# Entering the second graph layer of a four-layer network: paired projection, early aggregation, and float16 parts made elsewhere

## The chip, the cores and the metric

One core of one Trainium2 chip runs the whole program. The metric is device time in microseconds, from one launch. TensorE multiplies matrices, VectorE, ScalarE and GpSimd (POOL in the profile) do the elementwise work, SyncE (SP) issues most transfers. Each engine works through its own instruction list in order; they meet at semaphores.

## The reference

2048 nodes with 256 features; `adj` is a 2048 x 2048 matrix of zeros and ones. Four graph layers, each with a residual and a layer norm. The change lies between the first and the second:

```python
# layer 0: attention over the graph
e = where(adj > 0, h @ h.T, -9e15);  edge_att = softmax(e, axis=1)
x = layernorm(x + adj * (node_att * edge_att) @ (x @ weight) + bias)
# layer 1
type_sum = adj @ x                       # for both gates, and for (adj @ x) @ W_gcnb
attn_a, attn_b = sigmoid([type_sum, x] @ Wa.T + ba), sigmoid([type_sum, x] @ Wb.T + bb)
h = x @ W_sa
scores = (h @ a_left)[:, None] + (h @ a_right)[None, :]
e = where(adj != 0, exp(-leaky_relu(scores, 0.01)), 0)
x = layernorm(x + sigmoid(attn_a * (e / (e.sum(1) + 1e-5)) @ h + attn_b * (adj @ (x @ W_gcnb) + b_gcnb)))
# layers 2 and 3: two more graph convolutions, each with residual and layer norm
```

## The kernel before

**Numbers and parts.** A float32 product is made from a high and a low part of each operand (three products). `adjT`, the transposed adjacency, is bfloat16 and exact, so products with it need only the two parts of the other side. `x16` holds float16 high and low parts of 2048 times x.

**Layer 0, rounds of one row tile (128 rows, T = 16 tiles).** In round t (`round0`, `scores`, `weighted`) TensorE makes the 128 x 2048 scores in banks 0 to 3, VectorE adds the mask and takes the maxima in two halves (`maxima`, `masked_max`), ScalarE takes the exponential (`exp_row`) and the float16 high part of P (`p_high`), VectorE the low part (`p_low`), SyncE transposes both by DMA, and TensorE sums P times support (`weighted`) in bank 6 or 7, two rounds later. VectorE then does `final0` for tile t-3 (residual and moments), POOL the factor 1/sqrt(var) (`norm_factor`), VectorE the norm (`normed`), which gives the tile of x that layer 1 needs.

**The entry of layer 1.** Of each tile of x POOL makes the float16 high part (`conv_high`, line 455), VectorE the low part (`conv_first`, line 1183). TensorE transposes a pair of tiles (`turn16`, line 610, banks 4 and 5 in turn), ScalarE copies the result (`turned_read`, line 898; three kept), TensorE projects tile by tile (`project16`, line 625, banks 0 to 3): h, and in four more columns s_left, s_right and x's share of the two gates. ScalarE takes v = exp(-0.01 s_right) (line 902) and H_hi = v h (line 903), VectorE `ex` (line 1188) and H_lo (line 1189). A projection of tile t waits for both parts of tile t-4. When all 16 are through, `left_row` (line 637) spreads s_left over all partitions for 512 columns at a time, in banks 6 and 7.

**Layer 1 proper**, in four blocks b of 512 nodes. `aggregate_tiles` (line 664) adds adj times x over 16 tiles jt in banks 4 and 5 (4 matmuls a tile). Per pair of tiles: `edge_scores` on VectorE (lines 1278, 1281), two exponentials on ScalarE (`edge_exp`, lines 929, 930), `edge_low` on VectorE (line 1082), `attend` on TensorE (line 689, 24 matmuls). Each pair of attention has some aggregated tiles ahead of it; in block 0 that list is `AGG_FIRST = (8, 2, 2, 2, 1, 1)`, so all of block 0's aggregation stands behind the projection. After the sixth pair `neighbours` projects the aggregate.

**Memory.** `x16` lies over the adjacency's staging buffers `adjb` (high parts over buffers 0 and 1, low parts over 2 and 3), so conversions start only when the last mask (`fill_ready`, ScalarE's `make_fill`, line 850) and the adjacency's transposes are through.

**Orders written out by hand.** All of this stands in each engine's list in a fixed order. On POOL, `conv_high(0..6)` stands at the end of round t = 11 and 7..11 at the end of t = 12. POOL's and VectorE's rounds are those of tile t, which finishes three rounds of TensorE's later.

Of the kernel before, what the change touches and what calls it, by code (L numbers as in the profile page):

```python
# [23 lines left out]
ALU = mybir.AluOpType  # L24
# [46 lines left out]
def build(nc, x_in, adj_in, w0_in, b0_in, node_in, edge_in, wsa_in, asa_in, wg_in, bg_in,  # L71
# [31 lines left out]
    AGG_FIRST = (8, 2, 2, 2, 1, 1)  # L103
# [9 lines left out]
    with ctx:  # L113
# [193 lines left out]
        t16_mm, t16_read, sl_mm, sl_read = sem("t16_mm"), sem("t16_read"), sem("sl_mm"), sem("sl_read")  # L307
        p1_mm, p1_hi, p1_lo, ex_ready = sem("p1_mm"), sem("p1_hi"), sem("p1_lo"), sem("ex_ready")
# [93 lines left out]
        def _(pool):  # L402
# [45 lines left out]
            def conv_high(t):  # L448

                if t == 0:  # L450
                    pool.wait_ge(fill_ready, T)
                    for k in range(AB):
                        pool.wait_ge(adjT_landed[k], 16 * (T // AB))
# [68 lines left out]
        def _(pe):  # L522
# [78 lines left out]
            def turn16(g):  # L601

                pe.wait_ge(conv_lo, 2 * g + 2)
                if g >= 2:
                    pe.wait_ge(t16_read, g - 1)
                for i in range(2):
                    for part in (HI, LO):
                        for k in range(KD):
                            q = (2 * i + part) * KD + k
                            ins = nc.tensor.transpose(bank16(4 + g % 2)[:, q * P:(q + 1) * P],  # L610
                                                      x16[:, part, 2 * g + i, k * P:(k + 1) * P], identb[:, :])
                ins.then_inc(t16_mm, 1)

            def project16(t):

                if t == 0:
                    pe.wait_ge(w16_ready, 1)
                    pe.wait_ge(e_read, 2 * T)
                if t >= 4:
                    pe.wait_ge(p1_hi, t - 3)  # L620
                    pe.wait_ge(p1_lo, t - 3)
                pe.wait_ge(t16_read, t // 2 + 1)
                for k in range(KD):
                    for p, q in ((HI, HI), (HI, LO), (LO, HI)):
                        ins = mm(bank(t % 4, D + 4), turned16(t, p, k), w16[:, q, k, :],
                                 start=(k == 0 and (p, q) == (HI, HI)), stop=(k == KD - 1 and p == LO))
                ins.then_inc(p1_mm, 1)

            def left_row(b):

                if b == 0:
                    pe.wait_ge(p1_lo, T)
                    pe.wait_ge(pv_read, T)
                if b >= 2:
                    pe.wait_ge(sl_read, b - 1)
                for k in range(TB):
                    ins = nc.tensor.transpose(ps[:, 6 + b % 2, k * P:(k + 1) * P],
                                              ex[:, b * TB + k, 1:2].to_broadcast([P, P]), ident[:, :])
# [12 lines left out]
            left_row(0)  # L651
            left_row(1)
# [27 lines left out]

            def attend(b, pair):
# [17 lines left out]
            def block1(b):  # L699


                first, tiles = 0, AGG_TILES if b else AGG_FIRST
                wait_from(pe, g_ev, b * TB)
                for pair in range(PAIRS):
                    if pair < len(tiles):
                        for jt in range(first, first + tiles[pair]):
                            for f in range(KD):
                                aggregate_tiles(0, b, f, (jt,))
                            if b == 0 and jt == 3:
                                left_row(2)  # L710
                                left_row(3)
                        first += tiles[pair]
                    if b == 0 and pair == 0:
                        pe.wait_ge(H_ready, 2)
                    attend(b, pair)
# [5 lines left out]
            for k in range(AB):  # L721
                pe.wait_ge(adjT_landed[k], 16 * (T // AB))
# [106 lines left out]
        def _(act):  # L829
# [57 lines left out]
            for t in range(2, T):  # L887
                exp_row(t)
                p_high(t)
                if t + 2 < T:  # L890
                    make_fill(t + 2)
            def turned_read(g):
# [3 lines left out]
                if g >= KEPT:  # L896
                    act.wait_ge(p1_mm, 2 * (g - KEPT) + 2)
                run(xT16[:, g % KEPT, :], bank16(4 + g % 2), ACT.Copy).then_inc(t16_read, 1)

            def projected(t):  # L900
                act.wait_ge(p1_mm, t + 1)
                own.link(run(vj[:, t, :], ps[:, t % 4, D:D + 1], ACT.Exp, scale=gw[:, 4:5]))
                run(H[HI][:, t, 0:D], bank(t % 4, D), ACT.Copy, scale=vj[:, t, :]).then_inc(p1_hi, 1)

            def left_row(b):
                act.wait_ge(sl_mm, b + 1)
                run(slrow[:, b * CB:(b + 1) * CB], bank(6 + b % 2), ACT.Copy).then_inc(sl_read, 1)
# [58 lines left out]

            edge_exp(0, 0)
            left_row(2)
            left_row(3)
            edge_exp(0, 1)  # L970
# [99 lines left out]
        def _(dve):  # L1070
# [109 lines left out]
            def conv_first(tiles):  # L1180
                for t in tiles:
                    dve.wait_ge(conv_hi, t + 1)
# [3 lines left out]
            def projected(t):  # L1186
                dve.wait_ge(p1_hi, t + 1)
                own.link(ts(ex[:, t, :], ps[:, t % 4, D:D + 4], gw[:, 3:4], None, ALU.mult))
                stt(H[LO][:, t, 0:D], bank(t % 4, D), vj[:, t, :], H[HI][:, t, 0:D].bitcast(F32),
                    ALU.mult, ALU.subtract).then_inc(p1_lo, 1)  # L1190

            def round0(t):

                u = t % 2
                maxima(t, u)
                if t >= 3:
                    final0(t - 3, 1 - u)
                if t == T - 1:
                    conv_first(range(3))
# [55 lines left out]
            dve.wait_ge(H_ready, 1)  # L1255
            low(H[LO][:, :, D:D + 1], vj[:, :, :], H[HI][:, :, D:D + 1]).then_inc(H_ready, 1)
# [107 lines left out]
            for k in range(AB):  # L1364
                dve.wait_ge(adjT_landed[k], 16 * (T // AB))
            dve.wait_ge(sl_read, 1)
# [153 lines left out]
```

## Time and profile before

| | |
|---|---|
| runs (us) | 831.36, 829.05, 848.21; median 831.36 |
| profiled execution | 831.39 |
| its span, first to last instruction | 829.6 |
| TensorE busy | 775.2 (93%) |
| VectorE busy | 447.0 (54%) |
| ScalarE busy | 333.3 (40%) |
| POOL busy | 115.5 (14%) |
| mean granted clock of TensorE | 0.986 |

Times in rows are microseconds from the span's start. Layer 0 ends and layer 1 begins between about 204 and 260. Matmuls are pipelined: the duration of one includes its way through the array, so work is counted by the distance from one start to the next. In brackets stands an engine's idle time ahead of the instruction, and what ended it.

### The profile page before, as it was taken

How to read it: one execution, taken by the hardware profiler on the slowest of the kernel's cores; microseconds unless marked ns; L12 is line 12 of the kernel's file. 1: busy time of each engine (PE TensorE's matmuls, PEld its weight loads, DVE VectorE, ACT ScalarE, POOL GpSimd, SP SyncE). 2: the span in 40 equal slices, each digit the busy share in tenths (PEclk: the TensorE clock that was granted, in tenths of full speed). 3: DMA queues.
4: the chain of work that ended last, by engine and by line, in shares of the span. 5: the costliest groups of instructions: out<-in, count | busy, mean ns of one | idle time of the engine just before them, and what ended most of it. 6: DMA issues, size and time to landing. Idle time of an engine off the chain costs nothing.

```text
span 829.6 us, 11863 instructions
## 1 busy us (share of the span) xinstructions
PE 775.2 (93%) x4247; PEld 511.4 (62%) x4288; DVE 447.0 (54%) x937; ACT 333.3 (40%) x499; POOL 115.5 (14%) x214
## 2 busy tenths in 40 slices
PE   7898989899979999999979999999988999997997
PEld 6776656666656978686835554665663456464443
DVE  4586667477867778787873354221225111112655
ACT  4575536554465464646541142331335222223100
POOL 1012111112730001010111120000002000000343
PEclk9999999999989999999999999999999999999999
DMA  8979999995400000000011000000000000000011
GB/s 226 184 128 172 181 180 173 171 200 100 90 1 14 1 1 1 1 2 1 1 32 52 0 1 0 1 0 0 0 1 25 1 1 0 0 0 1 19 39 44
DMA packets 112572, 42.41 MB, mean 51 GB/s; under 512 B 103312, under 2 KB 109584, under 8 KB 112528
## 3 DMA queue, kind: packets, MB, share of 16 engines
q1 hardware_dynamic: 110224, 33.44, 20.6%
q0 software_dynamic: 2304, 8.39, 6.5%
q8 instruction: 27, 0.44, 0.2%
q14 instruction: 17, 0.14, 0.1%
HBM read 22.95 MB, written 2.10 MB: 30 GB/s over the span
## 4 chain that ended last, share of the span: by engine, by line
issue 40%; PE 35%; DVE 7%; SPq 6%; POOL 4%; DMA 4%; ACT 4%; POOLq 0%; ACTq 0%; DVEq 0%
PE ps L664 10%; PE ps L817 6%; PE ps L767 5%; SPq L365 4%; PE ps L571 3%; PE ps L754 3%; DMA turned<-pl 2%; PE ps L530 2%; SPq L358 2%; PE ps L583 2%; POOL rstd L417 1%; PE ps L553 1%; ACT em L855 1%; DVE em L1124 1%; PE ps L585 1%
## 5 line engine op out<-in xcount | busy, mean ns | idle before, releaser
L664 PE MATMUL ps<-adjT,x 128*128 128x512 bf16 (+1 forms) x739 | 168.5, 379 | 8.4 <-DVE x L1361 4.3
L664 PEld LDWEIGHTS ps<-adjT,x 128*128 128x128 f16 x768 | 71.8, 98 | 91.0 <-issue 5.6
L583 PE MATMUL ps<-sup,turned 128*128 128x512 f16 x256 | 85.7, 385 | 4.4 <-DMA turned<-pl 3.8
L1082 DVE TENSOR_TENSOR hh_lo<-hf,hh_hi 128x512 fp32r<-128x512 f32 x32 | 22.1, 692 | 116.6 <-ACT hf L1028 116.6
L789 PE MATMUL ps<-adjT,G 128*128 x375 | 82.6, 379 | 0.9 <-ACT hf L1028 0.4
L689 PE MATMUL ps<-H_hi,es_hi 128*128 128x258 f32 x256 | 76.8, 300 | 2.1 <-DVE es_lo L1082 1.7
L689 PE MATMUL ps<-H_hi,es_lo 128*128 128x258 f32 x256 | 72.4, 283 | 0.0
L689 PE MATMUL ps<-H_lo,es_hi 128*128 128x258 f32 x256 | 72.4, 283 | 0.0
L585 PE MATMUL ps<-sup,turned 128*128 128x256 f16 x256 | 70.6, 276 | 0.0
L416 POOL TENSOR_TENSOR rstd<-mv,epsc 128x1 f32<-128x1 f32 x64 | 14.6, 227 | 369.6 <-DVE mv L1096 361.8
L789 PEld LDWEIGHTS ps<-adjT,G 128*128 128x128 f16 x384 | 37.3, 98 | 45.4 <-issue 0.9
L817 PE MATMUL ps<-x,adjT 128*128 128x512 f16 x256 | 58.1, 387 | 3.7 <-DVE x L1465 3.7
L1133 DVE SCALAR_TENSOR_TENSOR pl<-em,ph 128x1024 f16<-128x1024 f32 x32 | 40.2, 1297 | 39.3 <-DMA turned<-pl 31.1
L571 PE MATMUL ps<-hT_hi 128*128 128x512 f32 x128 | 52.1, 407 | 6.1 <-DVE mx L1124 4.6
L855 ACT ACTIVATE em<-em,negm 128x2048 f32<-128x2048 f32 x16 | 32.1, 2004 | 63.8 <-DVE negm L1156 63.8
L929 ACT ACTIVATE es_hi<-tm 128x1024 fp32r<-128x1024 f32 x32 | 33.9, 1058 | 57.8 <-DVE tm L1281 55.7
L689 PEld LDWEIGHTS ps<-H_hi,es_hi 128*128 128x128 f32 x256 | 48.4, 189 | 6.8 <-DVE es_lo L1082 4.2
L571 PE MATMUL ps<-hT_hi,hT_lo 128*128 128x512 f32 x128 | 50.7, 396 | 0.0
L571 PE MATMUL ps<-hT_lo,hT_hi 128*128 128x512 f32 x128 | 50.4, 394 | 0.0
L689 PEld LDWEIGHTS ps<-H_lo,es_hi 128*128 128x128 f32 x256 | 48.5, 189 | 0.5
L583 PEld LDWEIGHTS ps<-sup,turned 128*128 128x128 f16 x256 | 25.3, 99 | 38.0 <-issue 9.3
L689 PEld LDWEIGHTS ps<-H_hi,es_lo 128*128 128x128 f32 x256 | 48.3, 189 | 0.0
(196 smaller groups left out, 1439.8 us busy)
## 6 DMA issues: line engine op xcount, KB each, us to landing
adjb<-in_adj POOLq DMA_DIRECT2D x16, 512.0 KB, 7.4
x<-in_x SPq DMA_DIRECT2D x4, 512.0 KB, 6.1
out<-adjf SPq DMA_DIRECT2D x16, 128.0 KB, 1.7
adjf<-in_L_gnn_W SPq DMA_DIRECT2D x1, 1024.0 KB, 5.4
W1f<-in_L_gnn_W SPq DMA_DIRECT2D x1, 512.0 KB, 3.7
adjf<-in_L_gnn_W SPq DMA_DIRECT2D x1, 512.0 KB, 3.8
we<-in_L_gnn_edge_w SPq DMA_DIRECT2D x1, 256.0 KB, 3.8
w0x<-in_L_gnn_weight SPq DMA_DIRECT2D x1, 256.0 KB, 7.0
```

What stands on the lines that cost most here:

```text
L365: sp.dma_start_transpose(PT(part, t % 2), (ph, pl)[part][:, :]).then_inc(PT_landed[part], 16)
L571: ins = mm(bank(c), hT[p][:, k, t * P:(t + 1) * P], hT[q][:, k, c * CB:(c + 1) * CB], start=(k == 0 and (p, q) == (HI, HI)), stop=(k == KD ...
L583: ins = mm(bank(6 + u), PT(HI, u)[:, jt, :], sup[:, jt, :], start=(jt == 0), stop=False, skip_group_check=True)
L585: ins = mm(bank(6 + u, D), PT(LO, u)[:, jt, :], sup[:, jt, 0:D], start=False, stop=(jt == T - 1), skip_group_check=True)
L664: ins = mm(bank(4 + f), x16[:, part, jt, f * P:(f + 1) * P], adj(b, jt), start=(jt == 0 and part == HI), stop=(jt == T - 1 and part == LO))
L689: ins = mm(bank(k, D + 2), es[p][:, (b * T + jt) % RE, k * P:(k + 1) * P], H[q][:, jt, :], start=(jt == 0 and (p, q) == (HI, HI)), stop=(j ...
L767: ins = mm(bank(2 + k % 2, width), hh[p][:, o, k * P:(k + 1) * P], ws[q][:, o, :], start=(o == 0 and (p, q) == (HI, HI)), stop=(o == KH - ...
L789: ins = mm(bank(4 + o), g16(jt, part, o * P, P), adj(b, jt), start=(jt == 0 and part == HI), stop=(jt == T - 1 and part == LO))
L817: ins = mm(bank(u), adjT[:, bass.ds(b, 1), jt, k * P:(k + 1) * P].rearrange("p a c -> p (a c)"), f16[:, jt, :], start=(jt == 0), stop=(jt ...
L855: run(em[:, t % 2, :], em[:, t % 2, :], ACT.Exp, bias=negm[:, t:t + 1], accum_out=Z[:, t:t + 1]) \
L929: own.link(run(es[HI][:, s, :], tm[:, s, :], ACT.Exp, scale=SLOPE - 1.0))
L1133: stt(pl[:, cols], em[:, u, cols], TOP, ph[:, cols], ALU.mult, ALU.subtract).then_inc(p_lo, 1)
```

## The change

1. **High parts.** Tiles 0 to 12 are converted by ScalarE: 0 to 6 after its last fill, 7 to 10 a round later, 11 and 12 after the last. POOL keeps 13 to 15, each right after its own tile's factor.
2. **Low parts** by VectorE: 0 to 2 between the halves of round 14's maxima, 3 and 4 before its P low part; 5 to 7 and 8 and 9 likewise in round 15; 10 to 15 among the last final steps.
3. **Projection in pairs** (`project16(g)`), with a semaphore `ex_made` for VectorE's columns. `projected(0)` and `projected(1)` stand earlier on VectorE. The last weighted sum stands after the first pair, not after the second.
4. **Early aggregation.** Between pairs, TensorE aggregates tiles 0 to 7 of block 0 (`agg_early`), so transposes go to banks 4, 5, 6, 6, 6, 7, 6, 6 (`TURN_BANK`). `AGG_FIRST` becomes (2, 2, 1, 1, 1, 1).
5. **Left row 0** is made after the fifth pair, and the first edge scores and exponentials of block 0 stand before the last projected parts on VectorE and ScalarE.

```diff
+    CONV_ROUND = {T - 2: (range(0, 3), range(3, 5)), T - 1: (range(5, 8), range(8, 10))}
+    TURN_BANK = (4, 5, 6, 6, 6, 7, 6, 6)
+    AGG_EARLY = 8
-    AGG_FIRST = (8, 2, 2, 2, 1, 1)
+    AGG_FIRST = (2, 2, 1, 1, 1, 1)
...
 # GpSimd
-                if t == T - 5:
-                    for c in range(7):
-                        conv_high(c)
-                if t == T - 4:
-                    for c in range(7, 12):
-                        conv_high(c)
                 if t >= T - 3:
-                    conv_high(t - 1)
-            conv_high(T - 1)
+                    conv_high(t)
...
 # TensorE, turn16
-                if g >= 2:
-                    pe.wait_ge(t16_read, g - 1)
+                if g == 2:
+                    pe.wait_ge(pv_read, T - 1)
+                if g == 5:
+                    pe.wait_ge(pv_read, T)
+                if to in TURN_BANK[:g]:
+                    pe.wait_ge(t16_read, max(n for n in range(g) if TURN_BANK[n] == to) + 1)
...
-            def project16(t):
+            def project16(g):
...
-                if t >= 4:
-                    pe.wait_ge(p1_hi, t - 3)
-                    pe.wait_ge(p1_lo, t - 3)
-                pe.wait_ge(t16_read, t // 2 + 1)
-                for k in range(KD):
+                if g >= 2:
+                    pe.wait_ge(p1_hi, 2 * g - 2)
+                    pe.wait_ge(p1_lo, 2 * g - 2)
+                    pe.wait_ge(ex_made, g - 1)
+                pe.wait_ge(t16_read, g + 1)
+                for t in (2 * g, 2 * g + 1):
...
             def left_row(b):
+                pe.wait_ge(ex_made, 2 * b + 2)
                 if b == 0:
-                    pe.wait_ge(p1_lo, T)
-                    pe.wait_ge(pv_read, T)
-                if b >= 2:
-                    pe.wait_ge(sl_read, b - 1)
+                    pe.wait_ge(t16_read, 6)
+                if b == 2:
+                    pe.wait_ge(t16_read, TURNS)
+                if b % 2:
+                    pe.wait_ge(sl_read, (b + 1) // 2)
...
-            weighted(T - 2)
-            turn16(0)
-            for g in range(1, TURNS):
-                if g == 3:
-                    weighted(T - 1)
-                turn16(g)
-                project16(2 * g - 2)
-                project16(2 * g - 1)
-            project16(T - 2)
-            project16(T - 1)
-            left_row(0)
-            left_row(1)
+            def agg_early(*jts):
+                for jt in jts:
+                    if jt == 0:
+                        pe.wait_ge(t16_read, 2)
+                        for k in range(AB):
+                            pe.wait_ge(adjT_landed[k], 16 * (T // AB))
+                    for f in range(KD):
+                        aggregate_tiles(0, 0, f, (jt,))
+
+            weighted(T - 2)
+            turn16(0)
+            turn16(1)
+            project16(0)
+            weighted(T - 1)
+            for g in range(1, TURNS - 1):
+                turn16(g + 1)
+                project16(g)
+                agg_early(g - 1)
+                if g == 4:
+                    left_row(0)
+            project16(TURNS - 1)
+            agg_early(TURNS - 2, TURNS - 1)
+            left_row(1)
...
 # TensorE, block1: left_row(2), left_row(3) stand before attend(0, 0), which also waits for p1_lo
...
 # ScalarE
+            def conv_high(tiles):
+                for t in tiles:
+                    if t == 0:
+                        act.wait_ge(fill_ready, T)
+                        for k in (0, 1):
+                            act.wait_ge(adjT_landed[k], 16 * (T // AB))
+                    act.wait_ge(y_normed, t + 1)
+                    run(x16[:, HI, t, :], x[:, t, :], ACT.Copy, scale=XS).then_inc(conv_hi, 1)
...
+                if t == T - 3:
+                    conv_high(range(7))
+                if t == T - 2:
+                    conv_high(range(7, 11))
+            conv_high(range(11, 13))
...
-            turned_read(0)
-            for g in range(1, TURNS):
-                turned_read(g)
-                projected(2 * g - 2)
-                projected(2 * g - 1)
-            projected(T - 2)
-            projected(T - 1)
-            run(H[HI][:, :, D:D + 1], vj[:, :, :], ACT.Copy).then_inc(H_ready, 1)
-            left_row(0)
-            left_row(1)
+            turned_read(0)
+            turned_read(1)
+            projected(0)
+            for g in range(1, TURNS - 1):
+                turned_read(g + 1)
+                projected(g)
+                if g == 4:
+                    left_row(0)
             edge_exp(0, 0)
+            projected(TURNS - 1)
+            column(0, T)
+            left_row(1)
+            edge_exp(0, 1)
             left_row(2)
             left_row(3)
-            edge_exp(0, 1)
...
 # VectorE
-            def maxima(t, u):
+            def maxima(t, u, between=()):
                 dve.wait_ge(fill_ready, t + 1)
                 masked_max(t, u, 0)
+                conv_first(between)
                 masked_max(t, u, 1)
...
+            def projected(g):
+                two, at = slice(2 * g, 2 * g + 2), 2 * (g % 2)
+                dve.wait_ge(p1_hi, 2 * g + 2)
+                ts(ex[:, two, :], ps[:, at:at + 2, D:D + 4], gw[:, 3:4], None, ALU.mult).then_inc(ex_made, 1)
+                for i in range(2):
+                    t = 2 * g + i
+                    stt(H[LO][:, t, 0:D], bank(at + i, D), vj[:, t, :], H[HI][:, t, 0:D].bitcast(F32),
+                        ALU.mult, ALU.subtract).then_inc(p1_lo, 1)
...
-            conv_first(range(3, 10))
+            conv_first(range(10, 12))
             final0(T - 3, 1)
-            conv_first(range(10, 12))
+            conv_first(range(12, 13))
             normed(T - 3, 1, x[:, T - 3, :])
-            conv_first(range(12, 13))
...
             final0(T - 2, 0)
             conv_first(range(13, 14))
+            projected(0)
             normed(T - 2, 0, x[:, T - 2, :])
-            for t in range(4):
-                projected(t)
+            conv_first(range(T - 2, T - 1))
             final0(T - 1, 1)
-            conv_first(range(T - 2, T - 1))
+            projected(1)
             normed(T - 1, 1, x[:, T - 1, :])
-            for t in range(4, 6):
-                projected(t)
+            projected(2)
             conv_first(range(T - 1, T))
-            for t in range(6, T):
-                projected(t)
+            for g in range(3, 6):
+                projected(g)
...
             dve.wait_ge(sl_read, 1)
             edge_scores(0, 0)
+            projected(TURNS - 2)
             edge_scores(0, 1)
+            projected(TURNS - 1)
+            dve.wait_ge(H_ready, 1)
+            low(H[LO][:, :, D:D + 1], vj[:, :, :], H[HI][:, :, D:D + 1]).then_inc(H_ready, 1)
```

## Rows read from the trace of the kernel before

**Rows 1.** The page's first part: busy time of each engine, share, instructions.

```profile
PE 775.2 (93%) x4247; PEld 511.4 (62%) x4288; DVE 447.0 (54%) x937; ACT 333.3 (40%) x499; POOL 115.5 (14%) x214
```

**Rows 2.** Busy time by stretch: length, engines' busy us, clock, DMA share, GB/s.

```profile
219.00:258.40 39.40, 32.51 (x244) 23.10 (x243) 26.56 (x77) 24.95 (x49) 12.92 (x16) 0.91 0.10 24
260.00:410.00 150.00, 147.06 (x1026) 121.08 (x1040) 124.00 (x232) 81.74 (x108) 11.69 (x24) 1.00 0.00 1
```

**Rows 3.** Timeline of TensorE, 219 to 262: start, busy, line, shapes, idle before.

```profile
219.45 1.06 PE L610 MATMUL ps<-identb,x 128*128 128x128 f16 x16
221.26 1.49 PE L625 MATMUL ps<-adjf,xT 128*128 128x260 f16 x12 [0.76 <-ACT xT L898]
222.59 0.61 PE L610 MATMUL ps<-identb,x 128*128 128x128 f16 x8
223.04 1.50 PE L625 MATMUL ps<-adjf,xT 128*128 128x260 f16 x12
224.37 0.38 PE L583 MATMUL ps<-sup,turned 128*128 128x512 f16 x1
...
229.57 0.61 PE L610 MATMUL ps<-identb,x 128*128 128x128 f16 x8
232.14 1.59 PE L625 MATMUL ps<-adjf,xT 128*128 128x260 f16 x12 [1.96 <-issue]
...
239.72 0.49 PE L625 MATMUL ps<-adjf,xT 128*128 128x260 f16 x3 [2.20 <-issue]
...
249.84 1.09 PE L637 MATMUL ps<-ident,ex 128*128 128x128 f32 x8 [1.83 <-DVE H_lo L1189]
250.98 3.40 PE L664 MATMUL ps<-adjT,x 128*128 128x512 bf16 x15
...
258.36 0.47 PE L689 MATMUL ps<-H_hi,es_hi 128*128 128x258 f32 x1
...
261.68 1.67 PE L664 MATMUL ps<-adjT,x 128*128 128x512 bf16 x7
```

**Rows 4.** Busy time by stretch, three more stretches; the third last column is the clock.

```profile
221.00:222.00 1.00, 0.74 (x7) 0.68 (x8) 0.93 (x3) 1.00 (x2) 0.92 (x2) 1.00 0.32 63
232.20:237.00 4.80, 4.80 (x34) 3.78 (x35) 3.73 (x12) 3.22 (x7) 0.51 (x2) 0.64 0.01 2
240.00:250.00 10.00, 8.08 (x65) 6.30 (x63) 7.17 (x23) 7.41 (x19) 3.32 (x2) 0.83 0.00 0
```

**Rows 5.** Timeline of VectorE before two of TensorE's pauses end.

```profile
230.64 0.42 DVE L1183 SCALAR_TENSOR_TENSOR x<-x 128x256 f16<-128x256 f32 x1 [1.89 <-POOL x L455]
...
231.56 0.48 DVE L1189 SCALAR_TENSOR_TENSOR H_lo<-ps,vj,H_hi 128x256 fp32r<-128x256 f32 x1
...
239.14 0.48 DVE L1189 SCALAR_TENSOR_TENSOR H_lo<-ps,vj,H_hi 128x256 fp32r<-128x256 f32 x1
```

**Rows 6.** Timeline, VectorE and ScalarE: rounds 14 and 15, and later conversions.

```profile
200.19 2.01 ACT L855 ACTIVATE em<-em,negm 128x2048 f32<-128x2048 f32 x1 [4.62 <-DVE negm L1156]
...
209.38 1.22 DVE L1124 CUSTOM_DVE_ANT_0 em<-ps,fill 128x1024 f32<-128x1024 f32 x1 [1.31 <-PE ps L571]
...
217.47 2.49 DVE L1183 SCALAR_TENSOR_TENSOR x<-x 128x256 f16<-128x256 f32 x6
...
495.51 1.38 ACT L981 ACTIVATE x<-x 128x256 f16<-128x256 f32 x4
```

**Rows 7.** Timeline, ScalarE and VectorE: copies, scaled copies, and one pair's edges.

```profile
220.09 1.94 ACT L898 ACTIVATE xT<-ps 128x1024 f16<-128x1024 f16 x2 [5.00 <-PE ps L610]
222.42 0.47 ACT L903 ACTIVATE H_hi<-ps,vj 128x256 fp32r<-128x256 f32 x1
...
251.72 1.42 DVE L1281 SCALAR_TENSOR_TENSOR tm<-slrow,ex,nb 128x512 f32<-128x512 f32 x2
...
253.17 1.06 ACT L929 ACTIVATE es_hi<-tm 128x1024 fp32r<-128x1024 f32 x1 [1.55 <-DVE tm L1281]
...
255.42 1.23 DVE L1082 TENSOR_TENSOR es_lo<-tm,es_hi 128x1024 fp32r<-128x1024 f32 x1 [0.37 <-ACT tm L930]
```

More of the change, by code:

```diff
@@ L448, in conv_high @@
             def conv_high(t):
[L450 to L453, printed above, removed]
                 pool.wait_ge(y_normed, t + 1)
@@ L609, in turn16 @@
                             q = (2 * i + part) * KD + k
-                            ins = nc.tensor.transpose(bank16(4 + g % 2)[:, q * P:(q + 1) * P],
+                            ins = nc.tensor.transpose(bank16(to)[:, q * P:(q + 1) * P],
                                                       x16[:, part, 2 * g + i, k * P:(k + 1) * P], identb[:, :])
                 ins.then_inc(t16_mm, 1)
-            def project16(t):
-                if t == 0:
+            def project16(g):
+                if g == 0:
@@ L627, in project16 @@
+                pe.wait_ge(t16_read, g + 1)
+                for t in (2 * g, 2 * g + 1):
+                    for k in range(KD):
+                        for p, q in ((HI, HI), (HI, LO), (LO, HI)):
+                            ins = mm(bank(t % 4, D + 4), turned16(t, p, k), w16[:, q, k, :],
+                                     start=(k == 0 and (p, q) == (HI, HI)), stop=(k == KD - 1 and p == LO))
                 ins.then_inc(p1_mm, 1)
             def left_row(b):
+                pe.wait_ge(ex_made, 2 * b + 2)
@@ L699, in block1 @@
             def block1(b):
-                first, tiles = 0, AGG_TILES if b else AGG_FIRST
+                first, tiles = (0, AGG_TILES) if b else (AGG_EARLY, AGG_FIRST)
                 wait_from(pe, g_ev, b * TB)
@@ L708, in block1 @@
                                 aggregate_tiles(0, b, f, (jt,))
-                            if b == 0 and jt == 3:
-                                left_row(2)
-                                left_row(3)
                         first += tiles[pair]
                     if b == 0 and pair == 0:
+                        left_row(2)
+                        left_row(3)
                         pe.wait_ge(H_ready, 2)
+                        pe.wait_ge(p1_lo, T)
                     attend(b, pair)
@@ L896, in turned_read, with column @@
                 if g >= KEPT:
[L897 to L903, printed above, removed]
+                    act.wait_ge(p1_mm, g - KEPT + 1)
+                run(xT16[:, g % KEPT, :], bank16(TURN_BANK[g]), ACT.Copy).then_inc(t16_read, 1)
+            def projected(g):
+                act.wait_ge(p1_mm, g + 1)
+                two, at = slice(2 * g, 2 * g + 2), 2 * (g % 2)
+                own.link(run(vj[:, two, :], ps[:, at:at + 2, D:D + 1], ACT.Exp, scale=gw[:, 4:5]))
+                for i in range(2):
+                    t = 2 * g + i
+                    run(H[HI][:, t, 0:D], bank(at + i, D), ACT.Copy, scale=vj[:, t, :]).then_inc(p1_hi, 1)
+            def column(first, last):
+                run(H[HI][:, first:last, D:D + 1], vj[:, first:last, :], ACT.Copy).then_inc(H_ready, 1)
             def left_row(b):
                 act.wait_ge(sl_mm, b + 1)
-                run(slrow[:, b * CB:(b + 1) * CB], bank(6 + b % 2), ACT.Copy).then_inc(sl_read, 1)
-            turned_read(0)
-            for g in range(1, TURNS):
-                turned_read(g)
-                projected(2 * g - 2)
-                projected(2 * g - 1)
-            projected(T - 2)
-            projected(T - 1)
-            run(H[HI][:, :, D:D + 1], vj[:, :, :], ACT.Copy).then_inc(H_ready, 1)
-            left_row(0)
-            left_row(1)
+                run(slrow[:, b * CB:(b + 1) * CB], bank(6 if b == 2 else 7), ACT.Copy).then_inc(sl_read, 1)
             def agg_high(layer, b, f):
@@ L1181, in conv_first @@
                 for t in tiles:
+                    if t == 0:
+                        dve.wait_ge(fill_ready, T)
+                        for k in (2, 3):
+                            dve.wait_ge(adjT_landed[k], 16 * (T // AB))
                     dve.wait_ge(conv_hi, t + 1)
@@ L1184, in conv_first, with projected @@
                         .then_inc(conv_lo, 1)
[L1186 to L1190, printed above, removed]
+            def projected(g):
+                two, at = slice(2 * g, 2 * g + 2), 2 * (g % 2)
+                dve.wait_ge(p1_hi, 2 * g + 2)
+                ts(ex[:, two, :], ps[:, at:at + 2, D:D + 4], gw[:, 3:4], None, ALU.mult).then_inc(ex_made, 1)
+                for i in range(2):
+                    t = 2 * g + i
+                    stt(H[LO][:, t, 0:D], bank(at + i, D), vj[:, t, :], H[HI][:, t, 0:D].bitcast(F32),
+                        ALU.mult, ALU.subtract).then_inc(p1_lo, 1)
             def round0(t):
                 u = t % 2
-                maxima(t, u)
+                maxima(t, u, CONV_ROUND.get(t, ((), ()))[0])
                 if t >= 3:
                     final0(t - 3, 1 - u)
-                if t == T - 1:
-                    conv_first(range(3))
+                conv_first(CONV_ROUND.get(t, ((), ()))[1])
                 p_low(t, u)
```

13 lines of the change are left out of this document (5 added, 8 removed).

## The prediction

> **What bounds the kernel now.** I first read the page's busy line [rows 1]: TensorE works 775.2 of 829.6 us, so time can only come from TensorE's own gaps or a slow clock. Then busy time by stretch [rows 2]. Between 260 and 410 us, the second layer, TensorE is busy 147.06 of 150 us while VectorE has 124.00: that stage is TensorE's, and what reaches it earlier leaves it earlier. In the 39.4 us before it TensorE is busy only 32.51, so I read that stretch instruction by instruction [rows 3], then with its clock [rows 4].
>
> The stretch runs from the first transpose (219.45) to the first attention matmul (258.36): 38.9 us. Its work at full clock, from start-to-start distances [rows 3]:
> - 8 groups of transposes at 0.45 (222.59 to 223.04): 3.6.
> - 16 projected tiles at 0.65 (12 matmuls, two tiles, from 221.26 to 222.59): 10.4.
> - The last row tile's weighted sum (224.37 to 229.57): 5.2.
> - 4 left rows: 8 transposes start at 249.84, the next work at 250.98, of which I count 0.95 as work: 1.9.
> - 8 aggregated tiles, 4 matmuls each at 0.213 (15 recorded in 3.40): 6.8.
>
> Together 27.9. So 11.0 us are lost. The pauses: 0.9 before 221.26, about 2.1 before 232.14, 2.3 before 239.72 and 1.9 before 249.84 (the rows count 0.76 to 2.20, from the end of the last matmul's way through the array; I count from where the next could have started): 7.2. The rest is clock: 0.64 granted over 4.8 us and 0.83 over 10 us, mixtures of the 1.2 and 2.4 GHz levels, are 1.7 and 1.7 us of lost work [rows 4], and 0.4 is in small waits. Each fall lies in the stretch behind one of the 2 us pauses; the 0.9 us pause is followed by none.
>
> What releases them is in VectorE's list [rows 5]. The pause before 232.14 ends with the first H_lo (231.56): VectorE does it only behind a float16 low part that waited 1.89 us for POOL, and the layer's norm behind that. The pause before 239.72 ends with the H_lo at 239.14, behind the last final step and a second such wait (two in all).
>
> **The change, part by part.** I laid each engine's new order end to end from 219.45 with these durations. The same laying out of the old order puts the first attention matmul at 256.8, or 258.4 with the part of the clock loss that isn't absorbed by waits; traced 258.36.
>
> *High parts to ScalarE.* POOL loses 13 of its 16 conversions. ScalarE makes 7 after its last fill, at the head of a wait of 4.62 us that begins at 195.6 [rows 6]. Four such conversions take 1.38 (495.51), so 7 take 2.5 and are ready at 198.1. Four follow the next p_high, inside the next wait; 11 and 12 after the last p_high, where ScalarE otherwise idles till 220.09. Cost 0, covered by ScalarE's waits; without them 13 x 0.35 = 4.5. The waits on the transposed adjacency move to ScalarE and VectorE and are long satisfied.
>
> *Low parts in the rounds.* Three stand between the halves of each of the last two maxima. VectorE waits there 1.31 us for the scores [rows 6], and 3 x 0.35 = 1.06 fits. Two more in each round stand before the low half of P, where VectorE waits for ScalarE. In the last round two replace three. So after that round VectorE has 2 to do instead of 7, which took 2.49 for six [rows 6]: final0(13) starts near 218.2 instead of 220.5. Bound if nothing is hidden: 1.06 us on the last maxima, which would reach only the last P tile. That tile's transposed low half stops moving at about 221.3 (DMA share 0.32 in that microsecond [rows 4]), and TensorE will want it at 222.6. Cover 1.3, cost 0.
>
> *TensorE's new head.* Transposes 0 and 1, project16(0) at 221.26 (same 0.9 pause, ScalarE's copy), and the last weighted sum already at 222.6 instead of 224.37, to 227.8.
>
> *VectorE and POOL beside it.* final0(13) to 220.6, low part 12, norm (POOL's factor costs 0.6 of wait), final0(14) to 224.5, low part 13, projected(0) to 225.9, norm 14, low part 14 after 1.0 of wait for POOL, final0(15) to 229.9. POOL's conversions 13 to 15 are in its queue right behind their factors, so both 1.9 us waits shrink, and what remains lies beside the weighted sum.
>
> *The alternation.* From 227.8 six groups: transpose, project a pair, aggregate one tile: 0.45 + 1.30 + 0.85 = 2.60. ScalarE needs 0.92 for the copy (two in 1.94, end to end) and 1.03 for a pair's exponential (0.29) and two scaled copies (0.47 alone, 0.37 back to back) [rows 7]: 1.95. VectorE needs 1.05. Every wait of TensorE is then met: bank 6 was copied 0.9 us before it is transposed into again, the parts of pair g-2 are ready before project16(g) by 1.5 or more. With left_row(0), the seventh pair at 243.9, tiles 6 and 7 and left_row(1): 247.4. No pause there, so I expect the full clock.
>
> *The first attention.* Two more tiles and two left rows bring TensorE to 250.1. What it needs: edge scores 1.9 on VectorE, of which 1.42 are the scores (242.9 to 244.8); exponentials 2 x 1.06 on ScalarE, to 246.9; there the last pair, to 248.2; VectorE's H_lo of it, to 249.2, the H column 0.12 and edge_low 1.23 [rows 7]: 250.5. It starts at 250.6, 7.8 before. In block 0, 10 tiles instead of 8 are aggregated ahead of it, so 2 x 0.85 = 1.7 less lies behind. VectorE's third edge_low is then just in time (259.05 against 259.0). **Sum 9.5.**
>
> *Not in any row:* the price of changing between projection and aggregation. Lower end 0, as from transposes to projection (222.59 to 223.04). Upper end, from the one long run of other matmuls: 24 of 258 columns take 3.32 from 258.36 to 261.68 [rows 3], and at the projection's 0.108 (260 columns) they would take 2.6, so at most 0.7 per change, 4.9 for seven inserted runs. I take 0.13 each, 0.9: the nearer rows are those that cost nothing, and the far one holds other things than the change. A gain is excluded: the matmuls of a group stay the same. Net **8.6 us**.
>
> The profiled execution took 831.39 (span 829.6 and 1.8 around it), and the median is 831.36, so no correction: 831.4 - 8.6 = 822.8.
>
> **A rule that speaks against it.** The rows say that short pauses leave the clock alone (0.9 us before 221.26, granted 1.00) and 2 us ones don't. The Trainium skill, "TensorE: Matmul & The Clock Gate", section "A second HAM failure mode: psum-queue depth-cycling", says that groups cycling through PSUM banks with micro-idles between them make the clock fall and rise repeatedly. This change cycles through banks 0 to 7 in small groups. By the rule the sum is that of rival 2; by the rows it is 822.8.
>
> **The rivals.**
> 1. *The pauses return in another form* (827.5). The pairs tie TensorE closer: project16(3) needs projected(1), which is behind final0(15) and so behind the last weighted sum. If POOL's answers come late by 2 us, a pause with a fall of the clock comes back (2.1 + 1.7), and if scores, both exponentials and the last pair run one after another behind the last projection, attention starts near 254, which leaves 6 of the 9.5; with one fall of the clock and the switching, 831.4 - 6 + 1.7 + 0.9 is 828, with a pause alone 827. For: VectorE and ScalarE do serve in strict order, and the third edge_low has no slack. Against: the laid-out slacks of 1.2 to 1.5.
> 2. *The clock falls through the alternation* (slower). Half clock over all 27 us from 222.6 to 250 would add 27 and leave 831.4 - 8.6 + 27 = 850. It decides from the point where 17 us of elapsed time are at half clock, which cancels 8.6; two falls as now cost 3.4 and leave 826. For: TensorE has many short waits there. Against: both falls in this stretch follow a pause of 2 us, and I lay out none over 0.9.
> 3. *Hidden anyway* (831). The gain would be lost if VectorE bounded the second layer. Against: 124 of 150 busy, and TensorE's busy 147 is not waiting. For: the third edge_low. I take this at 829 to 832.
> 4. *The last P tile lands late.* If the low parts between the maxima delay it by over 1.3, TensorE pauses before the weighted sum: 1 us more, 824, inside the forecast's range.
>
> **How the numbers follow.** Forecast with rival 4 (819 to 826): 0.66. Rival 1 (826 to 829): 0.17. Rival 3 and small losses (829 to 836): 0.11. Rival 2 beyond that: 0.05, of it 0.03 above 848. Better than 819: 0.01. The most there is to gain is the 11.0 lost now, 1.3%, so over 2% faster (below 814.7) is next to excluded: 0.01. Two per cent is about what a measurement of this kernel can tell from no change. Range: the switching price alone gives 821.9 (none) to 826.8 (all of it), the runs differ by a microsecond or two, and to leave out no more than 2 in 10 it takes in rival 1 and the near end of rival 3: 818.5 to 829.5.
>
> **What would show it.** In the changed profile: first transpose still near 219.4; the last weighted sum starts near 222.6; from there to 250 no pause of TensorE above 1 us and a granted clock of 1.00; transposes every 2.6 us; first attention matmul near 250.6; VectorE's waits for POOL near 1.0; the agg result of block 0 about 9 us earlier; from there the same distances as before. I am wrong if the clock is below 1.00 between 223 and 250, if TensorE waits for H_lo or for ScalarE's copies in each group, or if block 1 starts less than 7 us earlier.

## The result, and the profile after

The changed kernel took 825.57 us in the median of 6 runs (818.25 to 832.63), the kernel before 832.69 (828.92 to 848.21): ratio 0.9899, 95% interval 0.9856 to 0.9942, or 8.4 us less (4.8 to 12.0). The ratio and its interval leave out slow executions, those over 1.5% above the fastest of the same kernel, and so are not the quotient of the two medians. Forecast were 8.6 less and 822.8. A second set of runs gave 0.9899 again (0.9843 to 0.9955).

The page hides this. The profiled execution of the changed kernel is longer than that of before, 830.5 us of span against 829.6, so it has to be read by stretches. Layer 0 up to the last maxima is the same program in both, apart from the moved conversions, and took 10.7 us more. The waits of TensorE between 60 and 215 us of the two kernels, before first (waiting line, who ended it: us in total, times, longest), show where they went:

```profile
PE ps L571 <- DVE mx L1124: 4.1, 2, 3.1
PE ps L583 <- DMA turned<-pl: 3.8, 2, 2.1
```

and changed:

```profile
PE ps L577 <- DMA turned<-pl: 17.4, 3, 11.5
PE ps L565 <- DVE mx L1159: 0.7, 1, 0.7
```

TensorE waited 11.5 us for one transposed P tile; before, the longest such wait was 2.1. Whether that belongs to the change is settled by an experiment below. I therefore measure every run by a **distance** that leaves it out: from the second half of the last maxima on VectorE to the first aggregation matmul of block 1. Before it is 209.38 to 291.76, 82.4 us; changed, 220.08 to 292.51, 72.4. The changed kernel's starting point, on VectorE:

```profile
220.08 1.22 DVE L1159 CUSTOM_DVE_ANT_0 em<-ps,fill 128x1024 f32<-128x1024 f32 x1 [0.43 <-PE ps L565]
```

The other end needs a correction. Block 1 opens with 16 aggregation matmuls in every kernel. TensorE's timeline there, before:

```profile
291.41 0.28 PE L689 MATMUL ps<-H_hi,es_lo 128*128 128x258 f32 x1
291.76 3.40 PE L664 MATMUL ps<-adjT,x 128*128 128x512 bf16 x15
294.81 0.47 PE L689 MATMUL ps<-H_hi,es_hi 128*128 128x258 f32 x1
```

and changed:

```profile
292.39 0.28 PE L703 MATMUL ps<-H_hi,es_lo 128*128 128x258 f32 x1
292.51 3.63 PE L654 MATMUL ps<-adjT,x 128*128 128x512 bf16 x16
295.79 0.47 PE L703 MATMUL ps<-H_hi,es_hi 128*128 128x258 f32 x1
```

From the last attention matmul ahead of the run to the first one behind it is 3.40 in both, but before has 15 records, and they begin 0.35 behind the attention instead of 0.12. The record of the first matmul is missing, and block 1 began 0.23 earlier than the row says. Corrected, the distance before is 82.15 and the gain **9.7 us**. The same record is missing in six of the eleven profiles, those whose corrected distance in the table below is shorter. The starting point needs none: the first transpose stands 10.07 behind it before and 10.06 changed.

Here is TensorE between the maxima and block 1, in the timeline of the changed kernel; it answers to [rows 3], 10.7 us later in absolute time:

```profile
230.14 1.06 PE L609 MATMUL ps<-identb,x 128*128 128x128 f16 x16
231.96 1.49 PE L626 MATMUL ps<-adjf,xT 128*128 128x260 f16 x12 [0.76 <-ACT xT L926]
...
238.49 0.61 PE L609 MATMUL ps<-identb,x 128*128 128x128 f16 x8
238.93 1.50 PE L626 MATMUL ps<-adjf,xT 128*128 128x260 f16 x12
240.27 1.03 PE L654 MATMUL ps<-adjT,x 128*128 128x512 bf16 x4
241.13 0.61 PE L609 MATMUL ps<-identb,x 128*128 128x128 f16 x8
...
256.12 1.89 PE L654 MATMUL ps<-adjT,x 128*128 128x512 bf16 x8
257.84 0.60 PE L640 MATMUL ps<-ident,ex 128*128 128x128 f32 x4
...
260.01 1.04 PE L640 MATMUL ps<-ident,ex 128*128 128x128 f32 x8
261.13 0.36 PE L703 MATMUL ps<-H_hi,es_hi 128*128 128x258 f32 x1
...
292.51 3.63 PE L654 MATMUL ps<-adjT,x 128*128 128x512 bf16 x16
```

From the first transpose to the first attention matmul it is 31.0 us, where before it was 38.9. The only bracket is the 0.76 that was there before. Busy time by stretch, for the 39.4 us that answer to [rows 2], for 150 us of layer 1, and for the alternation alone (length, PE, PEld, DVE, ACT, POOL, clock, DMA share, GB/s):

```profile
229.70:269.10 39.40, 38.56 (x310) 28.91 (x309) 28.35 (x72) 25.97 (x45) 8.87 (x12) 1.00 0.11 24
270.70:420.70 150.00, 147.63 (x1044) 120.47 (x1044) 123.75 (x238) 83.19 (x119) 11.69 (x24) 1.00 0.00 1
238.40:261.10 22.70, 22.64 (x190) 16.60 (x189) 14.71 (x39) 18.77 (x34) 4.76 (x5) 1.00 0.01 2
```

TensorE is busy 38.56 instead of 32.51 at a clock of 1.00 instead of 0.91. Layer 1 behind it is as it was (147.63 of 150 us busy, 147.06 before), and from block 1 to the end it is 538.0 us, where before it was 537.8: what is gained is not given back there. VectorE's list answers to [rows 5 and 6]:

```profile
218.56 1.09 DVE L1223 SCALAR_TENSOR_TENSOR x<-x 128x256 f16<-128x256 f32 x3
...
238.22 0.43 DVE L1223 SCALAR_TENSOR_TENSOR x<-x 128x256 f16<-128x256 f32 x1 [0.98 <-POOL x L456]
...
241.78 0.87 DVE L1232 SCALAR_TENSOR_TENSOR H_lo<-ps,vj,H_hi 128x256 fp32r<-128x256 f32 x2
...
259.76 1.22 DVE L1117 TENSOR_TENSOR es_lo<-tm,es_hi 128x1024 fp32r<-128x1024 f32 x1
```

The three low parts took 1.09 between the maxima's halves, and the second half started 0.43 after them, still waiting for TensorE. One wait for a conversion of POOL's is left, of 0.98, and TensorE is in the last weighted sum meanwhile. ScalarE's seven and four conversions took 2.26 and 1.32, a little less than I had laid out for seven (2.5) and measured before for four (1.38):

```profile
206.30 2.26 ACT L903 ACTIVATE x<-x 128x256 f16<-128x256 f32 x7
214.99 1.32 ACT L903 ACTIVATE x<-x 128x256 f16<-128x256 f32 x4
```

### The profile page after: what moved, and what is told of

The parts are those of the page before. It is cut to its first block, busy times and chain, and to the rows that moved or that the text cites. A ratio compares the mean times of both kernels' runs of the same rounds, so it can differ in the third digit from the quotient of the medians.

```text
span 830.5 us, 11896 instructions
## 1 busy us (share of the span) xinstructions
PE 774.4 (93%) x4288; PEld 509.0 (61%) x4288; DVE 444.1 (53%) x929; ACT 335.5 (40%) x504; POOL 100.0 (12%) x201
## 4 chain that ended last, share of the span: by engine, by line
PE 41%; issue 38%; DMA 5%; SPq 4%; DVE 4%; ACT 4%; POOL 3%; POOLq 0%; ACTq 0%; DVEq 0%
PE ps L654 10%; PE ps L829 7%; PE ps L779 5%; PE ps L565 5%; PE ps L577 4%; SPq L370 4%; DMA turned<-pl 3%; PE ps L766 3%; PE ps L579 2%; PE ps L524 2%; PE ps L547 1%; ACT em L867 1%; POOL rstd L422 1%; DVE em L1159 1%; DMA x<-in_x 1%
## 5 line engine op out<-in xcount | busy, mean ns | idle before, releaser
L654 PE MATMUL ps<-adjT,x 128*128 128x512 bf16 (+1 forms) x768 | 174.6, 380 | 6.4 <-DVE x L1399 3.8
L577 PE MATMUL ps<-sup,turned 128*128 128x512 f16 x256 | 88.3, 393 | 18.1 <-DMA turned<-pl 17.4
L703 PE MATMUL ps<-H_hi,es_lo 128*128 128x258 f32 x256 | 72.5, 283 | 0.0
L703 PE MATMUL ps<-H_lo,es_hi 128*128 128x258 f32 x256 | 72.5, 283 | 0.0
L1168 DVE SCALAR_TENSOR_TENSOR pl<-em,ph 128x1024 f16<-128x1024 f32 x32 | 41.1, 1324 | 48.5 <-DMA turned<-pl 41.8
```

The costliest lines, as they stand in the source:

```text
L577: ins = mm(bank(6 + u), PT(HI, u)[:, jt, :], sup[:, jt, :], start=(jt == 0), stop=False, skip_group_check=True)
L654: ins = mm(bank(4 + f), x16[:, part, jt, f * P:(f + 1) * P], adj(b, jt), start=(jt == 0 and part == HI), stop=(jt == T - 1 and part == LO))
L703: ins = mm(bank(k, D + 2), es[p][:, (b * T + jt) % RE, k * P:(k + 1) * P], H[q][:, jt, :], start=(jt == 0 and (p, q) == (HI, HI)), stop=(j ...
L1168: stt(pl[:, cols], em[:, u, cols], TOP, ph[:, cols], ALU.mult, ALU.subtract).then_inc(p_lo, 1)
```

## The experiments

My theory: the change takes out pauses of TensorE and the clock falls behind them. Rival A: the gain is the aggregation that fills waits. Rival B: changing between kinds of matmul has a price. All distances, in us; "laid out" is what I wrote down before each run, and "corrected" takes off the 0.23 where the first record of block 1 is missing. What follows the distance, to the end of the program, was 537.3 to 539.1 in every one of these profiles, and the stretch ahead of it 207 to 221.

| kernel | last maxima | block 1 | distance | corrected | laid out | timed ratio (95%) |
|---|---|---|---|---|---|---|
| before | 209.38 | 291.76 | 82.4 | 82.15 | | |
| before, second profile | 207.32 | 290.38 | 83.1 | 82.8 | 79 to 82.4 | |
| before, third profile | 216.05 | 297.18 | 81.1 | 80.9 | 81 to 83 | |
| changed | 220.08 | 292.51 | 72.4 | 72.4 | 73.8 | 0.9899 (0.9856 to 0.9942) |
| changed, again | 217.27 | 289.73 | 72.5 | 72.5 | 72.4 | 0.9899 (0.9843 to 0.9955) |
| conversions alone | 207.49 | 283.37 | 75.9 | 75.9 | 76.0 | 0.9935 (0.9894 to 0.9975) |
| order alone | 221.14 | 298.05 | 76.9 | 76.9 | 76.6 or 78.3 | 0.9946 (0.9903 to 0.9989) |
| no alternation | 219.27 | 293.23 | 74.0 | 74.0 | 74.1 | 0.9913 (0.9874 to 0.9953) |
| transposes ahead | 208.37 | 280.45 | 72.1 | 71.9 | 71.5 | 0.9867 (0.9794 to 0.9939) |
| copies made twice | 207.78 | 282.55 | 74.8 | 74.5 | 74.7 | |
| low parts late | 207.31 | 280.06 | 72.8 | 72.5 | 72.6 | |

The 73.8 is 82.4 less the forecast's net of 8.6; its sum of 9.5, without the 0.9 that I added for switching, gives 72.9. The distances laid out for the later runs were reckoned from 82.4 and 72.4 as recorded. Each distance but the changed kernel's and the kernel's before is of one profile. The timed ratios order the kernels in the same way, but the intervals of any two of them overlap: it is the distances that tell them apart.

**The changed kernel again.** No edit.

> The changed kernel as it is. Measure for all runs: the distance from the last half of the last maxima on VectorE (starts 209.38 before, 220.08 in the changed kernel's first profile) to the first aggregation matmul of block 1: 82.4 before, 72.4 changed. My theory (the 9.9 us are TensorE's pauses and the clock falls behind them): again 72.4, ratio 0.988 to 0.990. Rival (the first profile's 10 us of waits for transposed P tiles in layer 0 belong to the change): the stretch up to the last maxima is again 10 us longer than before's 209.4. Mine: it varies by execution and comes out between 208 and 220.

The distance repeats within 0.03. The stretch ahead was again long (217.3). That it isn't the change's shows in the third profile of the kernel before, which has the same late tile:

```profile
PE ps L583 <- DMA turned<-pl: 12.3, 4, 10.2
PE ps L571 <- DVE mx L1124: 3.2, 2, 2.1
```

while two profiles with the changed kernel's rounds (transposes ahead, copies made twice) took 208.4 and 207.8. The 10 us come and go by execution in either kernel.

**Conversions alone**: the old order of TensorE, with POOL keeping 13 to 15.

```diff
+                if t == T - 3:
+                    conv_high(range(7))      # ScalarE; the rest as in the change
-                maxima(t, u)
+                maxima(t, u, CONV_ROUND.get(t, ((), ()))[0])
```

> The kernel before with only the conversions moved (ScalarE's high parts, low parts between the maxima). Mine: the wait of VectorE for POOL's conversions goes, so the pauses before projections 4 and 8 go with their falls of the clock, while the pause of 2 us before the left rows stays: distance 76.0, 6.4 less than before, ratio 0.992. Rival A (the gain is the aggregation filling TensorE's waits): moving conversions alone leaves the distance at 81 or more, ratio 0.999.

75.9: rival A is out as the whole cause. TensorE's waits from 217 us to the left rows:

```profile
PE ps L627 <- DVE H_lo L1200: 1.8, 1, 1.8
PE ps L615 <- ACT xT L904: 1.8, 3, 0.8
```

The pauses before projections 4 and 8 are gone, the one before the left rows (1.8) stays, and two short waits for ScalarE's copies, 1.0 in all, appear beside the old 0.76; before, VectorE was what TensorE waited for there. It is 6.3 less than before.

**Order alone**: the change with the conversions where they were.

```diff
-                if t >= T - 3:
-                    conv_high(t)
+                if t == T - 5:
+                    for c in range(7):
+                        conv_high(c)         # POOL, and 7 to 11, 12, ... as before
```

> The changed kernel with the conversions put back (POOL's high parts, low parts after the rounds). Mine: TensorE again waits for the low parts behind final0(15), one pause of about 3 us before the fourth pair, with a fall of the clock behind it: distance 76.6 without the fall, 78.3 with it, ratio 0.993 to 0.995. Rival A: the alternation gives nearly all, distance 73.5, ratio 0.989.

76.9, 5.2 less than before, so rival A fails here too (73.5). The pause is where it was laid out, before the fourth pair:

```profile
246.04 0.61 PE L620 MATMUL ps<-identb,x 128*128 128x128 f16 x8
249.74 1.49 PE L637 MATMUL ps<-adjf,xT 128*128 128x260 f16 x12 [3.10 <-DVE H_lo L1234]
```

But no fall of the clock followed it. These are the busy times of 8 us around it, and the clock stays at 1.00 in each microsecond from there to 271:

```profile
244.00:252.00 8.00, 4.90 (x42) 3.49 (x41) 5.09 (x17) 2.99 (x8) 3.40 (x6) 1.00 0.00 1
```

The halves give 6.3 and 5.2 and together 9.7, so they overlap by 1.8. Part of this is the clock: the first profile of the kernel before has a fall that costs 1.3 (below), and either half takes it out. Against the third profile, without that cost, they give 5.0 and 4.0 and together 8.5, and overlap by 0.5. That the rest is a wait for VectorE which each half shortens fits the order of the lists, but no run separates it.

**No alternation**: the eight early tiles behind left_row(1).

```diff
-                agg_early(g - 1)
...
-            agg_early(TURNS - 2, TURNS - 1)
             left_row(1)
+            agg_early(*range(TURNS))
```

> The changed kernel without alternation: the eight early tiles are aggregated in one run after the last pair and left_row(1). Mine: only short waits for ScalarE's copies come back (0.2 to 0.7 us each, 1.7 to 2.3 in all), no fall of the clock: distance 74.1, ratio 0.990. Rival A: the waits for copies and H parts come back in full, distance 79 or more. Rival B (changing between projection and aggregation has a price, up to 0.7 a change): the distance is shorter than the changed kernel's, under 72.

74.0. The alternation gives 1.5 of the 9.7. TensorE's waits are short ones, 0.4, 0.4 and 0.3 beside the old 0.8, and some too small to be listed. Rival B is out: the alternating order is the faster one.

**Transposes ahead.** Transposes 0 and 1 before the weighted sum of tile 14.

```diff
-            weighted(T - 2)
             turn16(0)
             turn16(1)
+            weighted(T - 2)
             project16(0)
```

> The changed kernel with transposes 0 and 1 before weighted(14) instead of behind it, so that ScalarE's copy of them lies beside the weighted sum. Mine: the one pause left (0.76 before the first projection) goes: distance 71.5 against 72.4, ratio 0.987. Rival (the last P tile's transposed low half, wanted 0.9 earlier, lands too late): a wait for it appears before the last weighted sum and the distance stays at 72.4.

The 0.76 is gone. But TensorE now comes to the last weighted sum before the transposed low half does:

```profile
219.33 1.50 PE L626 MATMUL ps<-adjf,xT 128*128 128x260 f16 x12
220.99 0.38 PE L577 MATMUL ps<-sup,turned 128*128 128x512 f16 x1 [0.16 <-DMA turned<-pl]
```

First attention comes 0.6 earlier than in the changed kernel (40.5 us after the maxima against 41.1), and block 1 too (71.9 corrected against 72.4). I had expected 0.9; the rival, a wait for the low half, took the other 0.3. By the profile this is the fastest of all versions; by timing it can't be told from the changed kernel.

**Copies made twice**, in `turned_read` from the third pair on.

```diff
+                if g >= 2:
+                    own.link(run(xT16[:, g % KEPT, :], bank16(TURN_BANK[g]), ACT.Copy))
                 run(xT16[:, g % KEPT, :], bank16(TURN_BANK[g]), ACT.Copy).then_inc(t16_read, 1)
```

> The changed kernel with ScalarE making its copy of each pair's transposes twice, one after the other, from the third pair on (1.06 us more for each of six). Mine: ScalarE needs 1.95 of the 2.6 us of a group and has 0.65 to spare, so only the rest shows, 0.3 to 0.8 us a group, 2.3 in all: distance 74.7. Rival (ScalarE has no part in it, TensorE's order has): 72.4. Rival (ScalarE's copies are already what sets the pace): 72.4 + 6.4 = 78.8.

74.5: of 6.4 us of added work 2.1 show, so ScalarE had about 0.7 us to spare in each group, and TensorE set the pace.

**Low parts late.** ScalarE's high parts stay; VectorE's go back.

```diff
-    CONV_ROUND = {T - 2: (range(0, 3), range(3, 5)), T - 1: (range(5, 8), range(8, 10))}
+    CONV_ROUND = {T - 1: (range(0), range(0, 3))}
...
-            conv_first(range(10, 12))
+            conv_first(range(3, 12))
```

> The changed kernel with ScalarE's high parts kept and only VectorE's low parts put back: 0 to 2 ahead of the last P low part, 3 to 11 behind the rounds, none between the maxima. Mine: what mattered in the conversions is that POOL is free for its factors; VectorE starts its final steps 2.4 us later but has about that much to spare, so one wait of 0.2 us appears: distance 72.6 against 72.4. Rival (VectorE's time between the maxima is what the conversions gain): the distance is 74.8, 2.4 more.

72.5, 0.1 more. The low parts between the maxima's halves are nearly without effect; of the 4.5 between the order alone and the changed kernel, ScalarE's high parts give the rest. By VectorE's list this is POOL's release: it waits 4.8 for POOL's conversions in the order alone, in four waits, and 0.98 here, in one.

**The kernel before, twice more**, for the clock.

> The kernel before once more, for its profile. Distance from the last maxima's second half to block 1's first aggregation. My theory so far (a pause of TensorE of 2 us is followed by a fall of the clock): 82.4 again, with the clock below 1.00 behind the pauses before projections 4 and 8. After the run with the conversions put back, whose 3.1 us pause was followed by no fall, the rival is that a fall behind such a pause comes in some executions only: then the distance lies between 79 and 82.4, shorter by up to 1.7 for each fall that is missing.

> The kernel before a third time, for its profile. By now: the pauses before projections 4 and 8 and before the left rows are fixed by VectorE and come again at the same distances; the falls of the clock behind them vary by execution (two in the first profile, one long one in the second). Distance 81 to 83.

The pauses come again at the same distances, the falls don't. The second profile misses what I had laid out: I took it that a missing fall shortens the distance, and this profile, with one fall instead of two, has the longest distance of the three. In the second profile the first pause (1.97) is followed by none, and the clock falls during the next pause of 3.9, while TensorE stands still, and stays low until 242.6; TensorE's timeline of that profile:

```profile
237.67 2.76 PE L625 MATMUL ps<-adjf,xT 128*128 128x260 f16 x12 [3.86 <-issue]
```

and the same profile by windows of 1 us (busy time of the five engines as above, clock, DMA share, GB/s), one within the pause and one behind it:

```profile
236.00:237.00 1.00, 0.00 (x0) 0.00 (x0) 0.83 (x3) 0.00 (x0) 0.13 (x1) 0.50 0.00 0
241.00:242.00 1.00, 1.00 (x8) 0.73 (x7) 0.70 (x2) 0.92 (x2) 0.34 (x1) 0.50 0.00 0
```

In the third only the first pause is followed by a fall. It cost nothing: the slowed projections eat into the next pause, which shrinks from 3.9 to 2.2, and projection 8 starts 30.36 us after the maxima, as in the first two profiles (30.34, 30.35). TensorE's timeline of the third:

```profile
238.83 2.64 PE L625 MATMUL ps<-adjf,xT 128*128 128x260 f16 x12 [1.99 <-issue]
...
246.41 1.50 PE L625 MATMUL ps<-adjf,xT 128*128 128x260 f16 x12 [2.21 <-issue]
```

So 80.9 is the distance with the clock out of it, and only a fall behind the second pause, or in it, costs: 1.3 in the first profile, 1.9 in the second, where the clock is low for longer (235.8 to 242.6, against 240.2 to 243.7).

## Why the prediction was right

*The bound and the place.* Right. The gain lies between the first transpose and block 1, layer 1's busy times are the same, and the part behind stays at 537.3 to 539.1 in all profiles.

*The laid-out order.* Right, step by step: the last weighted sum ends 8.35 after the first transpose (238.49 - 230.14; laid out 8.35), a group takes 2.64 (laid out 2.60), TensorE reaches the attention 31.0 after the first transpose (31.15), waiting about 0.2 us instead of 0.5. Up to the first attention it gains 7.9 (7.8), in block 0 1.8 (1.7). Sum 9.5, measured 9.7 against the first profile. The same arithmetic gave the distances of the six edited kernels within 0.4.

*The signs.* Those in absolute times didn't come: the first transpose is at 230.14 and not near 219.4, and block 1 begins 0.75 us later than before instead of 7 or more earlier, the sign named for being wrong. Read from the last maxima, which leaves out the wait in layer 0, they came, down to the result of block 0's aggregation, projected 9.7 earlier than before (63.7 after the maxima, and 73.5). The forecast had not asked how much layer 0 varies by execution, which moves everything behind it in a single profile: the last maxima start between 207.3 and 216.1 in the kernel before alone.

*High parts at no cost.* Right: seven took 2.26 inside ScalarE's wait, and VectorE's wait for POOL went from 1.89 to 0.98 and off the path.

*Low parts between the maxima.* Right that they cost nothing; I spoke of final0(13) starting 2.3 us earlier without asking what that was worth. It was worth 0.1. In the changed kernel projected(1) waits 0.65 for ScalarE, and its parts are there 1.6 before TensorE takes up the pair that needs them.

*The switching price.* The mis-sized term. I took 0.9 and measured none: from projection to aggregation 1.34 (238.93 to 240.27), as from projection to transposes before (1.33), and from aggregation to transposes 0.86 (240.27 to 241.13) for four matmuls of 0.213. The bound of 0.7 that I drew from the attention run was a misreading: 0.3 of it is the attention matmuls' own spacing (0.121 instead of 0.108), 0.23 a missing record (7 of 8 aggregation matmuls are recorded from 261.68 on), and the other 0.2 the early start of the attention's first record (0.31 ahead of the second).

*The clock.* The falls were the weakest term, and right only in sum. I counted 3.4 us of lost work as part of the 11.0. The third profile shows that the first fall cost nothing, because the pause behind it absorbs it, and the others that one behind the second pause costs 1.3 or 1.9 where it comes. I had booked 2.3 for the pause before projection 8 and 1.7 for the fall ahead of it; without the fall the pause itself is 3.9. The total was the same, so the forecast wasn't hurt. Averaged over three profiles of before (82.0) the change is worth 9.5, and 8.5 with the clock out of it; the timed 8.4 (4.8 to 12.0) holds both. That the net forecast of 8.6 lies so near the timed 8.4 is luck: the profiles give 8.5 to 10.3, by what the clock does in the kernel before, and the net had 0.9 in it for a price that isn't there.

*The rule that spoke against it.* In the alternation the granted clock is 1.00 throughout, and so it is in the order alone with its 3.1 us pause and in the copies made twice, so rival 2 is out. The Trainium skill ("TensorE: Matmul & The Clock Gate", section "A second HAM failure mode: psum-queue depth-cycling") reports a kernel whose groups of matmuls cycle through PSUM banks and in which small waits between them made the clock go up and down; this trace, with the same pattern, does not agree: its clock stayed at 1.00.

*The other rivals.* Rival 1 didn't come: no pause above 0.8. (Its price for a pause alone was added wrongly: 831.4 - 6 + 0.9 is 826.3 and not 827.) But its mechanism is the order alone, where the fourth pair waits 3.1 us behind final0(15): the two halves of the change need each other. Rival 3 is out (layer 1 passes on the gain, within the 2 us by which the part behind varies). Rival 4 didn't occur, but the cover against it was mis-sized. I had taken the point where the transposed low half stops moving, and 1.3 of cover. In the transposes-ahead run the DMA share is 0.86 from 220.0 to 220.5 and 0.00 in the half microsecond behind, yet TensorE goes on only at 220.99, 12.6 after the last maxima. In the changed kernel it wants the tile at 13.2: a cover of 0.6.

*The absolute time.* The median of 825.57 is above 822.8 although the difference was right, since the kernel before had 832.69 in the shared runs and not 831.36. With late tiles of 10 us in some executions, three runs don't fix a base to better than a few microseconds.

## What to carry to other kernels

Lay each engine's instruction list end to end with durations from the trace, old order first as a check, then the new: the forecast's sum and six later layouts came within 0.4 us here, while timing could not tell any two of the variants apart. Count the records before reading a distance: one missing matmul shifted six of eleven distances by 0.23. A fall of the clock ahead of a later, fixed wait cost nothing here, so count to the next fixed point instead of adding up lost work. When two executions of nearly the same program differ, split the span at points that both have before explaining anything.

## What was unexpected of the hardware

- The clock falls behind similar pauses in some executions only. Behind the 2.0 us pause before projection 4 it fell in two of three profiles; with the longer one that follows (2.2 to 3.9), in two of three, once already during the pause; behind the 3.1 us pause in the order alone not at all; behind the 1.8 us pause before the left rows in none of four.
- The DMA transposes of layer 0 kept TensorE waiting between 2.1 (low parts late) and 17.8 us (order alone) in executions of nearly the same rounds. What makes them late was not tried.
